# Loads in a six-phase transformer kernel: inputs right behind three quantised weights, the other weights issued by ScalarE, clearing without a wait for the constants

## The reference

```python
x = x + 0.5 * lora_ffn(layernorm(x))        # "f": top-1 of 8 experts by LoRA, 128 -> 512 -> 128
x = x + linear_attention(layernorm(x))      # "a": 16 heads of 8
x = x + 0.5 * lora_ffn(layernorm(x))        # "f"
x = x + 0.5 * fp4_ffn(layernorm(x))         # "g": silu(gate) * up, then down
x = x + nystrom_attention(layernorm(x))     # "n": 64 landmarks, 6 steps of an iterated inverse
x = x + 0.5 * fp4_ffn(layernorm(x))         # "g"
```

## Time and profile before

| | us |
|---|---|
| median of three timed runs | 2108.1 |
| lowest and highest of them | 2106.43 and 2112.0 |
| profiled execution | 2111.74 |
| its span, from first to last instruction | 2109.5 |
| TensorE busy (share of span) | 1866.0 (88%) |
| VectorE busy | 1657.2 (79%) |
| ScalarE busy | 1100.0 (52%) |
| GpSimd busy | 855.5 (41%) |

### The profile page before, as it was taken

The page is one execution under the profiler, slowest core; times in us unless marked ns, Lnnn a source line. Parts: engine busy times, 40 slices in busy tenths (PEclk is TensorE's granted clock), DMA queues, the critical chain, the costliest instruction groups (busy, mean ns, idle before and its releaser), DMA issues.

```text
span 2109.5 us, 66299 instructions
## 1 busy us (share of the span) xinstructions
PE 1866.0 (88%) x27657; PEld 1442.1 (68%) x27657; DVE 1657.2 (79%) x3936; ACT 1100.0 (52%) x2880; POOL 855.5 (41%) x913
## 2 busy tenths in 40 slices
PE   0999899999799778868999999999999999957885
PEld 0888566666688556656777777777777777745664
DVE  5566688888666699975888888888888888759995
ACT  0344333333244466645666666666666666536662
POOL 2000477777100056533444444444444444425563
PEclk9999899999999999987999999999999999979998
DMA  4000000000000000000000000000000000000002
GB/s 114 1 1 1 1 2 2 2 2 2 1 1 1 1 1 1 1 1 2 3 3 3 3 3 3 3 3 3 3 3 3 3 3 3 3 1 1 1 1 80
DMA packets 14553, 14.45 MB, mean 7 GB/s; under 512 B 1392, under 2 KB 12080, under 8 KB 14256
## 3 DMA queue, kind: packets, MB, share of 16 engines
q1 hardware_dynamic: 14256, 10.20, 1.8%
HBM read 6.01 MB, written 4.19 MB: 5 GB/s over the span
## 4 chain that ended last, share of the span: by engine, by line
PE 69%; DVE 22%; issue 6%; ACT 2%; POOL 1%; SPq 0%; DVEq 0%; DMA 0%; POOLq 0%
PE acc L472 6%; PE acc L1653 5%; PE acc L449 5%; PE acc L1643 5%; DVE arena L899 4%; PE acc L749 4%; PE acc L1665 4%; PE acc L767 3%; DVE acc L886 3%; DVE arena L876 2%; PE acc L1695 2%; PE acc L463 2%; PE acc L1593 2%; PE acc L1681 2%; PE acc L1576 2%
## 5 line engine op out<-in xcount | busy, mean ns | idle before, releaser
L1493 POOL TENSOR_TENSOR arena<-arena 128x288 f32<-128x288 f32 (+1 forms) x384 | 291.9, 766 | 460.4 <-ACT arena L1400 400.0
L1400 ACT ACTIVATE arena<-acc 64x288 f32<-64x288 f32 x384 | 155.4, 405 | 142.5 <-PE acc L1671 135.1
L1219 DVE SCALAR_TENSOR_TENSOR arena<-acc,arena 128x288 f32<-128x288 f32 (+1 forms) x384 | 157.1, 409 | 71.9 <-PE acc L1665 39.4
L923 POOL TENSOR_TENSOR arena<-arena 128x960 f32<-128x960 f32 (+2 forms) x74 | 119.9, 1620 | 203.6 <-DVE arena L892 203.6
L935 POOL TENSOR_TENSOR arena<-arena 128x960 f32<-128x960 f32 (+2 forms) x74 | 119.2, 1611 | 175.3 <-DVE arena L902 143.9
L667 POOL TENSOR_TENSOR arena<-arena,quadcol 128x512 f32<-128x512 f32 x64 | 65.2, 1040 | 289.8 <-DVE arena L545 289.8
L424 ACT ACTIVATE arena<-acc,wib 128x256 f32<-128x256 f32 x256 | 100.3, 475 | 149.6 <-PE acc L463 149.6
L1006 PE MATMUL acc<-wguT,arena 128*128 128x352 f32 x256 | 104.8, 492 | 74.5 <-DVE arena L876 73.6
L1653 PE MATMUL acc<-arena 64*64 64x72 f32 (+1 forms) x3072 | 134.2, 224 | 13.0 <-DVE arena L1210 12.7
L1665 PE MATMUL acc<-arena 64*64 64x72 f32 (+1 forms) x3072 | 135.2, 224 | 11.7 <-DVE arena L1219 11.6
L1653 PEld LDWEIGHTS acc<-arena 64*64 64x64 f32 x3072 | 111.8, 135 | 46.7 <-issue 44.0
(11 more groups left out here) (241 smaller groups left out, 4971.9 us busy)
## 6 DMA issues: line engine op xcount, KB each, us to landing
out_dram<-X SPq DMA_DIRECT2D x4, 1024.0 KB, 9.3
wi<-in_wiT_dram SPq DMA_DIRECT2D x1, 256.0 KB, 2.6
wout<-in_woT_dram SPq DMA_DIRECT2D x1, 256.0 KB, 3.2
wqkv<-in_w_qkv_dram SPq DMA_DIRECT2D x1, 192.0 KB, 2.7
arena<-in_w_down_dram SPq DMA_DIRECT2D x1, 176.0 KB, 2.4
arena<-in_w_gate_dram SPq DMA_DIRECT2D x1, 128.0 KB, 2.2
arena<-in_w_up_dram SPq DMA_DIRECT2D x1, 128.0 KB, 2.3
wq<-in_WqT_dram SPq DMA_DIRECT2D x1, 64.0 KB, 2.3
```

The lines of the kernel that those rows point to most:

```text
L923: pool.tensor_tensor(b3(y[k][:, part(u)]), b3(z[k][:, part(u)]), each(small[u % kept][:, 1, blocks(u)]), ALU.mult).then_inc(y_ready, 1)
L1219: dve.scalar_tensor_tensor(pm[s][:, group[g], cols], pn[s][:, group[g], cols], part, tm[s][:, group[g], cols], ALU.mult, ALU.add).then_inc ...
L1400: ins = act.mul(sq[s][rows, group[g], :], pn[s][other, group[g], 0:MW], part)
L1493: pool.tensor_tensor(tm[s][:, group[g], cols], pm[s][:, group[g], cols], sq[s][:, group[g], cols], ALU.subtract).then_inc(tm_ready, 1)
```

## The change

It has four parts. VectorE no longer waits for `masks` at its start, but behind the statistics. The three large loads of the quantised weights and the four quarters of X are issued by SyncE without a wait. ScalarE waits for the clearing, issues the two short tails of w_gate and w_up (the last 96 rows of each), and then the other 18 weight loads, those of the first phase first. VectorE's quantising waits for a semaphore of its own, `given`, which counts the five loads of the three weights; the wait for all others and the halving of wo_b stand behind the statistics.

```diff
@@ prepare() @@
-                dve.wait_ge(loaded, 16 * N_LOADS[0])
-
-                chain.did(dve.tensor_scalar(wob[:, :], wob[:, :], 0.5, None, ALU.mult))
+                dve.wait_ge(given, 16 * 5)
...
                             dve.wait_ge(x_loaded[c], 16)
                             dve.bn_stats(bn[:, tile, :], X[:, tile, :])
+                dve.wait_ge(masks, 1)
+                dve.wait_ge(loaded, 16 * N_LOADS[0])
+                chain.did(dve.tensor_scalar(wob[:, :], wob[:, :], 0.5, None, ALU.mult))
...
@@ macaron_kernel() @@
-        loads = []
-        for base, w in ((0, w_gate), (3, w_up)):
-            loads.append((prepare.rows[:, base:base + 2, :], w[0:2 * P, :].rearrange("(t p) d -> p t d", p=P)))
-            loads.append((prepare.rows[0:FH - 2 * P, base + 2, :], w[2 * P:FH, :]))
-        loads += [(prepare.drow[:, 0, :], w_down), (wq[:, :], WqT), (wk[:, :], WkT), (wkv[:, 0:D], WkT),
...
+        loads = [(wgl[:, 0:NE], gateT), (wgl[:, NE:NE + ER], loraA),
+                 (wi[:, :], wiT), (wib[:, :], wi_b.rearrange("(f p) -> p f", p=P)),
...
         @block.sync
         def _(sp):
-            sp.wait_ge(prepare.zeroed, 2)
-            with nc.allow_non_contiguous_dma(reason="a bias of 512 values by partition, once"):
-                for dst, src in loads:
-                    sp.dma_start(dst, src).then_inc(loaded, 16)
+            for base, w in ((0, w_gate), (3, w_up)):
+                sp.dma_start(prepare.rows[:, base:base + 2, :], w[0:2 * P, :].rearrange("(t p) d -> p t d", p=P))\
+                    .then_inc(prepare.given, 16)
+            sp.dma_start(prepare.drow[:, 0, :], w_down).then_inc(prepare.given, 16)
             for c in range(QUARTERS):
                 sp.dma_start(X[:, quarter[c], :], xt[:, quarter[c], :]).then_inc(x_loaded[c], 16)
...
         @block.vector
         def _(dve):
-            dve.wait_ge(masks, 1)
             for f in vec:
                 f(dve)
...
         @block.scalar
         def _(act):
+            act.wait_ge(prepare.zeroed, 2)
+            for base, w in ((0, w_gate), (3, w_up)):
+                act.dma_start(prepare.rows[0:FH - 2 * P, base + 2, :], w[2 * P:FH, :]).then_inc(prepare.given, 16)
+            with nc.allow_non_contiguous_dma(reason="a bias of 512 values by partition, once"):
+                for dst, src in loads:
+                    act.dma_start(dst, src).then_inc(loaded, 16)
             for f in sca:
                 f(act)
```

More of the change, by code:

```diff
@@ L195, in prepare @@
             small = cut(3 * (6 * P // BLK))
-            quantized, turned, turned_out, zeroed = (
-                sem(f"prep_{n}") for n in ("quantized", "turned", "turned_out", "zeroed"))
-            prepare.rows, prepare.drow, prepare.zeroed = rows, drow, zeroed
+            quantized, turned, turned_out, zeroed, given = (
+                sem(f"prep_{n}") for n in ("quantized", "turned", "turned_out", "zeroed", "given"))
+            prepare.rows, prepare.drow, prepare.zeroed, prepare.given = rows, drow, zeroed, given
             def v(dve):
@@ L1832, in macaron_kernel @@
         quarter = [slice(c * NT // QUARTERS, (c + 1) * NT // QUARTERS) for c in range(QUARTERS)]
-        loads = []
-        for base, w in ((0, w_gate), (3, w_up)):
-            loads.append((prepare.rows[:, base:base + 2, :], w[0:2 * P, :].rearrange("(t p) d -> p t d", p=P)))
-            loads.append((prepare.rows[0:FH - 2 * P, base + 2, :], w[2 * P:FH, :]))
-        loads += [(prepare.drow[:, 0, :], w_down), (wq[:, :], WqT), (wk[:, :], WkT), (wkv[:, 0:D], WkT),
[L1838 to L1842, removed]
+        loads = [(wgl[:, 0:NE], gateT), (wgl[:, NE:NE + ER], loraA),
+                 (wi[:, :], wiT), (wib[:, :], wi_b.rearrange("(f p) -> p f", p=P)),
+                 (wout[:, :, :], woT.rearrange("(f p) d -> p f d", p=P)), (wob[:, :], across(wo_b, D)),
+                 *[(wlb[ER * f:ER * f + ER, :], loraB[:, f * P:(f + 1) * P]) for f in range(FT)],
+                 (gbias[:, :], across(gate_b, NE)),
+                 (wq[:, :], WqT), (wk[:, :], WkT), (wkv[:, 0:D], WkT), (wkv[:, D:2 * D], WvT), (wo[:, :], WoT),
+                 (wqkv[:, :], w_qkv), (wproj[:, :], w_proj)]
         N_LOADS[0] = len(loads)
```

## The result

| | before | changed |
|---|---|---|
| median of six timed runs each, us | 2109.2 | 2088.54 |
| lowest and highest | 2106.43, 2112.0 | 2088.09, 2093.05 |
| profiled execution, span | 2111.74, 2109.5 | 2088.09, 2085.9 |
| first norm instruction | 46.31 | 30.35 |
| TensorE's first normalised tile | 50.36 | 34.40 |

The ratio of changed to before is 0.9908, 95% interval 0.9895 to 0.9921. One execution of the kernel before took 3513.76 us in that later measurement; it is left out of every comparison.

What follows compares the result with a forecast made beforehand. TensorE bounds the kernel, idle at the head behind a one-engine-at-a-time chain; the first norm moves from 46.31 to 29.7 us (4.6 + 11.33 + 1.0 + 12.46 + 0.2 + 0.12). Forecast: 2108.1 - 16.6 = 2091.5 us, range 2087 to 2100.

Steps and rivals of the forecast that it cites:

- The start of the quantising: Head of kernel, VectorE: quantising starts at 4.6 us instead of 22.40, 17.8 earlier; bounds 4.1 to 8.8.
- Overlap with GpSimd: VectorE's quantising, now beside GpSimd's constants and copies, grows by 1.0 us, range 0 to 2.4.
- The moved halving and the statistics: Before the first norm: statistics unchanged at 12.46 us, wo_b's halving behind them adds 0.2, gap of 0.12 stays.
- X in time: Head loads: X's last quarter lands at 24 us, wanted by the statistics at 26.3; cover 2 us, the thinnest.
- rival A: Head transfers become the bound, X's last quarter lands near 29.4: gain 13.5, time 2094.6; chance 0.22 with C's mild form.
- ScalarE's work: Head: ScalarE's twenty load issues run 1.2 to 10.8 us, weights land in time with cover 5 or more; cost nothing.
- B: Head: the tails wait behind X, norm at 48.1 us, time 2110; chance 0.04 including other outcomes within 0.3%.
- C: Head: queued X pushes back ScalarE's issues, up to 3.14 us each, norm 17.4 later, time 2125; chance 0.02.

Runs made afterwards that it cites:

- that later measurement: The unmodified changed kernel measured once more beside the kernel before on one chip: 2089.9 us against 2108.6, ratio 0.9915.

## Why the prediction was right

**The start of the quantising** was put at 4.6, measured 4.72. The tails came first, as reckoned; w_down took 2.9 us to land, not 2.3, beside its four neighbours.

**Overlap with GpSimd** was put at 1.0 us, measured 1.58, inside the bounds 0 to 2.4; holding GpSimd back gave 11.34. This is the largest miss of the sum. The row it was sized by, L1210 with a mean loss of 0.15, was of instructions that meet GpSimd only part of the time; its median is 428 ns against the mean of 561. Here four of w_down's instructions (L82, L84, L86 and L88) lost 0.28 to 0.29 each beside the four large copies, 1.15 us together, and a small one (L74) lost 0.24; the rest lost 0.18 between them. Two of the four, L82 and L84, have a single input. The 2.4 us that the prediction reckoned as one full copy for each of four were too much: each copy stood in the way for about half its length. That GpSimd would be held up was right, by 3.4 us; TensorE's transposes waited for it, from 12.0 to 12.17, and nothing else did.

**The moved halving and the statistics:** 12.46 as before, and 0.26 from their end (30.09) to the norm, for 0.32 reckoned (0.2 + 0.12). With the start and the overlap this gives the norm at 30.35 for the forecast 29.7, 15.96 us earlier for 16.6.

**X in time:** right, and the cover of 2 us too, in part by two misses that cancel. The full rate of 290 GB/s was over by 24, as worked out, but the transfers thinned out behind it (156 GB/s in 23:24, 18 in 24:25) and the last quarter landed at 25.0, not at 24. It was wanted at 26.98, not at 26.3, as the quantising took longer. The third quarter was not safer, as the text has it: it landed at 21.7 for 23.8, a cover of 2.1. With GpSimd held back the same quarter landed at 26.55 and the statistics stopped for 0.89 us. So the cover is real but no more than a faster quantising and one late execution use up, and there rival A's wait appears, at 0.9 us and not at 3.

**ScalarE's work:** 20 issues took 1.25 to 12.06, not to 10.8, and a weight landed 7.5 us after its issue at the median, not 2.5. Both were covered as said: the last weight landed at 22.6, and was wanted at 30.0.

**Rivals B and C:** B's mechanism is real in a weaker form (7.4 us for a tail behind X's issues), and was absent since the tails went first. C's push-back of ScalarE's issues was small: in the changed kernel the longest was 1.09 us, for wo_b, and the four of loraB took 2.12 together, far from 2.25 each.

**The 3 us by which the median fell below the forecast** are no step of the sum. 15.7 us at equal clock is the norm's 16.0. The rest goes with TensorE's mean granted clock in the runs compared; with 40 and 12 runs the means are 17.1 apart, and 17.9 side by side, nearer to the forecast 16.6 than the first medians' 20.7. For the first six runs of the kernel before the clock of only one is on record (0.970), so for them this is argued from the slope, not shown. Why the clock differs between executions stays open.

## To carry to other kernels

At the head of a kernel, follow the one chain that leads to the bound engine's first work, and ask of each link whether the next one needs it: half the gain here was a wait that ordered nothing; the other half was a wait for 23 loads where five were needed, and X's place in the queue (in which shares is only estimated above). Small loads that something waits for are issued before the large one. Issued beside it by a second engine they took three times as long to land (7.5 us for 2.3); issued behind it by the same engine they went out only when its four issues were over, some 10 us later. Work whose result is wanted late (here the weights' quantising) is better spread where its engine idles than moved up at the head. Compare kernels at equal granted clock where a fraction of a per cent matters.

## What the runs showed of the hardware

- A small load issued by ScalarE beside 1 MB quarters in flight lands 7.5 us after its issue at the median (the changed kernel's 18 weights) instead of 2.3; the four X issues take 14.0 us with another engine issuing and 10.0 without.
- The full rate ends before the last quarter of X lands: 289 GB/s in 22:23, 156 in 23:24 and landing at 25.0 in the changed kernel; 295 in 22:23, 98 in 23:24, 29 in 25:26 and landing at 26.55 with GpSimd held back.
- VectorE and GpSimd slow each other: four GpSimd copies of 32x4 took 0.89 us together when alone, 2.88 beside VectorE's 128x768 instructions. Of VectorE's, a 128x352 tensor_scalar with one input (0.34 to 0.63) lost as much as a tensor_tensor with two (0.53 to 0.81). The statistics (one input) kept their 0.195 us each with GpSimd working beside them.
- The same instructions of the fifth phase took 933.8 us in one execution and 940.5 in another, with TensorE's granted clock at 0.50 for longer after the phase's start. Over all kernels 0.001 of mean granted clock goes with 1.3 us in 2100.
